# Windowed attention on one core: the softmax reciprocals go through GpSimd's DMA queue instead of SyncE's, the query loads move ahead of the key stores, and the block numbers are read one step earlier

## The reference, cut to what matters

```
logits = qd * SCALE @ jnp.swapaxes(kd, -1, -2)          # window means against window means
topk_logit, r_idx = jax.lax.top_k(logits, TOPK)         # TOPK = 4 block numbers for each window
kv_sel = kv_pix[jnp.arange(N)[:, None, None], r_idx]    # keys and values of those four windows
attn = jnp.einsum('npqhd,npkhd->nphqk', qh * SCALE, kh)
attn = jax.nn.softmax(attn, axis=-1)                    # over 4 * 64 keys
out = jnp.einsum('nphqk,npkhd->npqhd', attn, vh)
out = out + lepe                                        # a 3x3 depthwise convolution of v
out = out @ wo_w + wo_b
```

## Time and profile before

| | |
|---|---|
| median of three runs | 4997.75 us |
| the profiled execution | 4994.8 us, span 4993.0 us |
| attention with its loop | up to about 3640 us of the span |
| TensorE busy | 3844.4 us (77%), granted clock 0.86 on the mean |
| VectorE, ScalarE, GpSimd busy | 2436.6 (49%), 2310.0 (46%), 1249.2 us (25%) |
| DMA engines' mean busy share | between 0.2 and 0.5 in the attention |

### The profile page before, as it was taken

How to read it: one execution, slowest core, us unless ns; L and a number is a source line. 1 busy time by engine, 2 the same in 40 slices (tenths; PEclk the granted TensorE clock), 3 DMA queues, 4 the chain that set the end, 5 groups by cost and what they waited for, 6 DMA issues and landing times. The chain is left out here.

```text
span 4993.0 us, 164000 instructions
## 1 busy us (share of the span) xinstructions
PE 3844.4 (77%) x52926; PEld 2709.4 (54%) x52926; DVE 2436.6 (49%) x4011; ACT 2310.0 (46%) x5133; POOL 1249.2 (25%) x4158
## 2 busy tenths in 40 slices
PE   4246688678778777876877877788949799999889
PEld 1124455455445545544544554456612388888789
DVE  2254575475457447555745754576625233333311
ACT  1125565565556655555655555567713233333300
POOL 1012343243234324333432433344400000000000
PEclk9998898898888889888888888899955699999955
DMA  2323334333333333333333433343259543444486
GB/s 77 106 59 100 94 90 100 100 94 91 95 99 90 100 96 95 89 99 95 91 99 95 96 92 98 95 95 68 41 75 142 89 106 85 106 95 95 102 183 166
DMA packets 778337, 484.80 MB, mean 97 GB/s; under 512 B 483370, under 2 KB 752043, under 8 KB 773131
## 3 DMA queue, kind: packets, MB, share of 16 engines
q1 hardware_dynamic: 718210, 407.83, 36.5%
q10 hardware_dynamic: 59360, 67.44, 4.6%
HBM read 264.35 MB, written 209.19 MB: 95 GB/s over the span
## 5 line engine op out<-in xcount | busy, mean ns | idle before, releaser
L552 POOL COPY Ksel<-Kexp 96x128 int32 x3136 | 908.9, 332 | 1895.4 <-PE ps L1173 1406.8
L908 DVE TENSOR_REDUCE Mx<-ps 128x2 f32<-128x512 f32 x1568 | 1063.7, 688 | 526.7 <-PE ps L1151 520.3
L751 ACT ACTIVATE Pr<-ps 128x1024 f32<-128x1024 f32 x784 | 800.6, 1021 | 797.6 <-PE ps L1173 770.8
L681 ACT ACTIVATE Vsel<-Vpx 64x72 f32 x3136 | 818.3, 261 | 278.3 <-issue 144.1
L1171 PE MATMUL ps<-Qbd,Ksel 96*128 96x128 bf16 x6272 | 873.9, 229 | 21.2 <-issue 19.6
L1173 PE MATMUL ps<-MT,each 84*128 84x128 bf16 x6272 | 874.4, 229 | 0.0
L1151 PE MATMUL ps<-Ksel,Qbd 96*128 96x256 bf16 x3136 | 649.7, 291 | 170.3 <-POOL Ksel L552 125.5
L1171 PEld LDWEIGHTS ps<-Qbd,Ksel 96*128 96x128 bf16 x6272 | 646.2, 103 | 96.9 <-issue 87.6
L1173 PEld LDWEIGHTS ps<-MT,each 84*128 84x128 bf16 x6272 | 647.4, 103 | 90.4 <-issue 82.2
L1190 PE MATMUL ps<-Pr,Vsel 128*9 128x64 f32 x25088 | 538.2, 230 | 109.4 <-ACT O L689 99.6
L1190 PEld LDWEIGHTS ps<-Pr,Vsel 128*9 128x9 f32 x25088 | 392.2, 95 | 303.2 <-issue 302.1
(11 more groups left out here) (166 smaller groups left out, 3848.5 us busy)
## 6 DMA issues: line engine op xcount, KB each, us to landing
q_dram<-Pq SPq DMA_DIRECT2D x336, 112.0 KB
k_dram<-Pk SPq DMA_DIRECT2D x336, 112.0 KB
Kexp<-k_dram ACTq DMA_DIRECT2D x112, 336.0 KB, 5.2
Qbd<-q_dram SPq DMA_DIRECT2D x224, 168.0 KB, 4.8
Vpx<-v_dram ACTq DMA_DIRECT2D x112, 252.0 KB
s_dram<-S SPq DMA_DIRECT2D x8, 2048.0 KB, 12.7
Sin<-s_dram SPq DMA_DIRECT2D x32, 512.0 KB, 5.7
z_dram<-Zs SPq DMA_DIRECT2D x128, 128.0 KB, 4.1
```

Source lines behind the costliest of these rows:

```text
L552: nc.gpsimd.tensor_copy(dst[:, w, :, k, :], src[:, :, bass.ds(win[k] * (PX // 2), PX // 2)])\
L681: nc.scalar.activation(Vsel[par][half, w, k // 2], Vpx[b][half, bass.ds(win[k], 1)], ACT.Copy).then_inc(v_gathered, 1)
L751: nc.scalar.activation(Pr[k][:].rearrange("q c p h x -> q (c p h x)"), ps[:, ST0 + 2 * k:ST0 + 2 * k + 2, :].rearrange("q a b -> q (a b)") ...
L908: nc.vector.tensor_reduce(Mx[u % 2][:, 2 * half:2 * half + 2, w], ps[:, half, :].rearrange("q (p k) -> q p k", p=2), AX.X, ALU.max).then_i ...
```

## The change

Three edits, all in the attention:

* Steps 4 and 5 of the chain leave SyncE's program and stand in GpSimd's: the store after the gather of w = 2, the four loads ahead of the gather of w = 4 (behind `square`, ahead of `square2` and of the split of w = 5). SyncE's `sums_spread` now waits for the landing of the store of the unit before (`rsums_out`).
* In SyncE's slot `load_q` and `load_x` stand ahead of `store_k`.
* The register loads are functions of their own (`fetch_k`, `fetch_v`) and stand ahead of the wait for `st_ready`; on ScalarE that is also ahead of the exponential.

```
@@ sync engine @@
             def sums_spread(g, m):
                 hold(sp, "sp", o_copied, g * 2 + 2)
-                hold(sp, "sp", rsums_ready, g)
+                hold(sp, "sp", rsums_out, g * 16)
...
                 if behind:
                     store_q(e, u - 1)
-                if prev:
-                    rsums_to_dram(g - 1, (u - 1) % 2)
                 if behind:
                     store_vs(e, u - 1)
...
-                if behind:
-                    store_k(e, u - 1)
-                if prev:
-                    rsums_spread(g - 1, (u - 1) % 2)
                 if u < UNITS - 2:
                     hold(sp, "sp", st_ready, g * NWIN)
                     load_q(d, u + 2)
                 if not last and u < LAST:
                     load_x(e, u + 1)
+                if behind:
+                    store_k(e, u - 1)
@@ gpsimd @@
+            def fetch_k(u, w):
+                pool.load(regs, idxrow[0:1, u // NWIN, bass.ds((u % NWIN * NWIN + w) * TOPK, TOPK)])
+
+            def rsums_to_dram(g, m):
+                hold(pool, "pool", rsums_ready, g + 1)
+                pool.dma_start(rsums_dram[m].rearrange("j (p x) -> (j p) x", p=32), rsums[:, :]).then_inc(rsums_out, 16)
+
+            def rsums_spread(g, m):
+                hold(pool, "pool", rsums_out, g * 16 + 16)
+                hold(pool, "pool", on_ready, g)
+                for j in range(4):
+                    pool.dma_start(Rb[32 * j:32 * j + HD, :], rsums_dram[m, j].partition_broadcast(HD))\
+                        .then_inc(rb_loaded, 16)
...
+                    if w == 4 and prev:
+                        rsums_spread(g - 1, (u - 1) % 2)
...
+                        fetch_k((u + 2) % UNITS, w)
                         hold(pool, "pool", st_ready, g * NWIN + w + 1)
                         gather_k((u + 2) % UNITS, w)
+                    if w == 2 and prev:
+                        rsums_to_dram(g - 1, (u - 1) % 2)
                     if w == 3 and u <= LAST and not last:
                         square(e * NWIN + u, e * NWIN - 9 + min(u, 2))
                     if w == 4 and load is not None:
                         square2(load[0] * NWIN + load[1], e * NWIN + (0 if last else min(u, LAST) + 1))
@@ scalar engine @@
+                        fetch_v((u + 1) % UNITS, w)
                     hold(act, "act", st_ready, g * NWIN + w + 1)
                     hold(act, "act", pv_done, g * NWIN + w - 1)
...
```

More of the change, by code:

```diff
@@ L512, in _ @@
             sums_spread(duos * UNITS - 1, 1)
-            rsums_to_dram(duos * UNITS - 1, 1)
-            rsums_spread(duos * UNITS - 1, 1)
             store_u(d, NWIN - 2)
@@ L548, in gather_k @@
                 dst = Ksel[u % 2][:, :, :, :, :].bitcast(I32)
-                pool.load(regs, idxrow[0:1, b, bass.ds((u % NWIN * NWIN + w) * TOPK, TOPK)])
                 win = [pool.snap(r, min_val=0, max_val=WINDOWS - 1) for r in regs]
@@ L575, in _ @@
                 for w in range(NWIN):
+                    fetch_k(u, w)
                     gather_k(u, w)
@@ L583, in slot @@
                 load = late(d, u, first)
+                prev = not (first and u == 0)
                 for w in range(NWIN):
@@ L607, in _ @@
             bodies(pool, body)
+            rsums_to_dram(duos * UNITS - 1, 1)
             square2(tiles - 2, tiles)
+            rsums_spread(duos * UNITS - 1, 1)
             square2(tiles - 1, tiles)
@@ L671, in keep_v, with fetch_v @@
                                      ACT.Identity, bias=bv[:, 0:1]).then_inc(vs_ready, 1)
+            def fetch_v(u, w):
+                act.load(regs, idxrow[0:1, u // NWIN, bass.ds((u % NWIN * NWIN + w) * TOPK, TOPK)])
             def gather_v(g, u, w):
@@ L676, in gather_v @@
                 hold(act, "act", pv_done, (g - 2) * NWIN + w + 1)
-                act.load(regs, idxrow[0:1, b, bass.ds((u % NWIN * NWIN + w) * TOPK, TOPK)])
                 win = [act.snap(r, min_val=0, max_val=WINDOWS - 1) for r in regs]
@@ L725, in _ @@
             for w in range(NWIN):
+                fetch_v(0, w)
                 gather_v(0, 0, w)
@@ L747, in slot @@
                         inv_std2(load[0] * NWIN + load[1])
+                    if not (last and u == UNITS - 1):
+                        if w == 0 and u + 1 == NWIN:
+                            hold(act, "act", v_loaded[1], d * (16 * NWIN) + 16 * NWIN)
+                            hold(act, "act", idx_stored[1], d * 16 + 16)
+                        if w == 0 and u + 1 == UNITS:
+                            hold(act, "act", v_loaded[0], e * (16 * NWIN) + 16 * NWIN)
+                            hold(act, "act", idx_stored[0], e * 16 + 16)
+                        fetch_v((u + 1) % UNITS, w)
                     hold(act, "act", st_ready, g * NWIN + w + 1)
@@ L760, in slot @@
                     if not (last and u == UNITS - 1):
-                        if w == 0 and u + 1 == NWIN:
-                            hold(act, "act", v_loaded[1], d * (16 * NWIN) + 16 * NWIN)
-                            hold(act, "act", idx_stored[1], d * 16 + 16)
-                        if w == 0 and u + 1 == UNITS:
-                            hold(act, "act", v_loaded[0], e * (16 * NWIN) + 16 * NWIN)
-                            hold(act, "act", idx_stored[0], e * 16 + 16)
                         gather_v(g + 1, (u + 1) % UNITS, w)
```

## The result

The changed kernel takes 5225.31 us (median of four runs, 5217.19 to 5237.27) against 4998.07 for the kernel before: ratio 1.0449, 95% interval 1.0426 to 1.0472. It is 227 us slower where 138 faster was forecast, outside the range.

A forecast was written before the change was run, and what follows sets the result against it. TensorE was the engine to fill, with 49 storing units waiting for a late `Rb` behind key stores. 280 + 25 - 127 - 9 - 30 - 3 = 136 us gained, so 4860 us; 8 in 10 range 4680 to 5060.

The forecast's parts named there:

- The store has long landed (1771.1 + 1.35): Storing units: the reciprocals' store, issued by GpSimd until 1771.1, lands 1.35 us later, before the broadcast loads start at 1773.9.
- On a queue of their own they don't stand behind them, and I take 2.4: Storing units: broadcast loads, no longer behind the key stores, land 2.4 us after their last issue instead of 5.66.
- the rival of the DMA engines: Loads limited by the DMA engines, not their queue place: landing keeps 5.66 us, time about 5020; chance 0.12.
- c = 0.9: Price in us of one DMA issue on GpSimd; a tenth moves 50 us, and the sign turns at 1.17.
- rival of cheap issues: A DMA issue on GpSimd costs about 0.5 us, storing units hit their ceiling, time about 4705; chance 0.22.
- c would be near 0.7 and the sum some 70 us better: Price of a GpSimd issue if set only by the skill's first-byte times, about 1 us against 0.6.
- 3.1 us a unit: 41 late units with a second layer norm: GpSimd's store and loads delay `square2`, which TensorE's `variance2` awaits; 127 us lost.
- costed at nothing: Query and band loads ahead of the key stores, and register loads ahead of the waits, were given no cost.
- neither load is waited for now: SyncE's query and band loads: nothing waits for them in the kernel before, so moving them was given no cost.
- u = 8 and the last duo: Quiet u = 8 without a layer norm loses 1.3 us in 7 units, 9 us; the last duo loses 30 us.
- the stated alarm: The prediction is wrong outright if `Rb` still lands over 5 us after its last issue.
- interleaving is what puts four small transfers ahead of the rest of six large ones: Argument that on shared DMA engines the four broadcast loads pass the six key stores, against landing staying 5.66 us.

The follow-up runs named there:

- pool_bulk_behind: The changed kernel with SyncE's twelve query and key stores held back until that unit's reciprocals' store has landed, query loads in front; 5463.27 us.
- bulk_last: The kernel before, chain still on SyncE, with `store_q`, `store_vs` and `store_k` behind the chain, the query loads and the band load; 5199.13 us.
- spread_first: The kernel before with the four broadcast loads ahead of the six key stores in SyncE's queue; 4899.44 us.
- pool_only: The kernel before with only the reciprocals' store and broadcast loads moved to GpSimd's queue; query loads and register loads where they were; 5165.24 us.
- pool_and_loads: The kernel before with the chain moved to GpSimd and the query and band loads ahead of the key stores, without the register-load edit; 5154.71 us.
- after_band_later: The changed kernel with ScalarE issuing the load of a band of keys at w = 4 and not at w = 3; 5123.89 us.

## Why the prediction was wrong, point by point

- **"The store has long landed (1771.1 + 1.35)": failed, and it is the step that decided the sign together with the next.** 1.35 us was read in the quiet unit and carried into the storing ones. There the store starts 1.9 to 3.3 us after the last of the six query stores is issued, and it lands in 5.5 to 7.1 us (means of u = 1 to 7). With the stores held back it lands in 2.0 to 3.7 (pool_bulk_behind), issued by SyncE with the stores behind it in 1.3 to 2.1 (bulk_last, u = 1 to 6). The query stores ahead of it are not the whole of this: in spread_first they stand there too, and it is 2.4 to 4.5. Nor is it the query loads, since pool_only, where they come later, has 6.0 to 7.2. What the kernels on GpSimd add, the transfers that SyncE issues behind the store or GpSimd's own queue, was not separated. The trace of before already had the term: the store's own data packets end 2.9 to 4.4 us after its issue in storing units and 0.7 us after it in u = 10, and its list has SyncE waiting for this landing after 5 us of key stores.

```profile
SPq L285 <- DMA rsums_dram<-rsums: 76.5, 57, 3.0
```

- **"On a queue of their own they don't stand behind them, and I take 2.4": failed.** The landing after the last issue stayed at 5.2 to 5.4 us in five of the seven storing units, on their means (3.5 in u = 2, 4.6 in u = 7; before 5.4 to 5.8), which is the rival of the DMA engines. The working had the key stores start at about 1771 and the loads at 1773.9, so the key stores were first in it too; it counted only places in a queue. The 2.08 us of the earlier trace rows was right for quiet stretches: in the last duo of the changed kernel, where VectorE waits, it is 1.7 to 2.5. This rival's own sum, 5020, was still 205 us too low, since it left the store's landing at 1.35.
- The unit u = 4 closes with these terms. From the end of the store's issue to VectorE's start I had 8.8 us (1771.1 to 1779.9). The store landed 4.3 us later than GpSimd was ready for it by my working (7.1 against 2.8), the four issues took 2.0 instead of 3.6, and `Rb` landed in 5.8 instead of 2.4: 8.8 + 4.3 - 1.6 + 3.4 = 14.9, as measured.
- **c = 0.9: wrong in the good direction.** The row of the kernel after:

```profile
L548 POOL DMA_DIRECT2D Rb<-rsums_dram x448: 502/507/547, 374.0 to 3860.3; - x150
L542 POOL DMA_DIRECT2D rsums_dram<-rsums x112: 589/598/752, 366.9 to 3856.3; - x112
```

  An issue costs 0.51 us, near SyncE's 0.34 and not near a tensor operation. My rival of cheap issues had this right, and with it forecast 4705 (its own sum gives 4709): the cheapness was worth little, since in both units above the store's landing, and not the issues, decided when the loads could go. The text's "c would be near 0.7 and the sum some 70 us better" is mis-summed too: at its own 50 us a tenth that is about 100.
- **Late units, "3.1 us a unit": the mechanism held, the size did not.** TensorE waits for `square2` as said (4.30 us in u = 10, forecast about 3.5), and moving the loads behind it returns 117 us there. The price was 197 instead of 127 us: the store, "landed 1962.6" by the same 1.35 us, needs 3.0 to 3.6 us to land from GpSimd in u = 9 to 12 (1.9 to 2.0 with the band's load later, 1.3 to 1.6 from SyncE); and behind the gap TensorE runs on at half the clock.
- **What is late next, once one stall is gone:** I named no successor to the wait for `Rb` inside GpSimd. The split of the maxima follows the loads in its queue, and TensorE's transposition waits 173.2 us for it.
- **Register loads "costed at nothing": right alone, wrong together.** The text had them compete with the exponential; what they did was to let a 336 KB load past the store. Query loads at nothing: right (pool_only 5165, pool_and_loads 5155), though "neither load is waited for now" was not: the list of before has TensorE waiting for `Qbd` for 38.2 us in 8 cases (29.9 in the kernel after).
- u = 8 and the last duo: 23 and 44 us against 9 and 30. I put this down to the same two causes; no run was made for it.
- Of what would show it, the stated alarm came: `Rb` over 5 us after its last issue. The late units did lengthen (u = 10 to 29.8 us, about 27 forecast), and TensorE's wait for the product fell below 150 (131.7). Storing units at 28 us, and the wait for `Rb` under 250, did not come.

The Trainium skill (DMA: Bandwidth & Descriptors, Issuing engines are not separate DMA queues) says that DMAs of all engines run on the same 16 DMA engines and interleave. The landings agree: 5.2 to 5.4 us from GpSimd's queue, 5.4 to 5.8 from SyncE's behind six key stores. My argument against the rule, that "interleaving is what puts four small transfers ahead of the rest of six large ones", did not hold here: four small loads issued on another queue after the key stores landed hardly sooner than on the same queue, and much sooner only where the key stores were issued behind them (2.9 to 3.4 us in u = 2 of the change, 2.1 to 3.1 in spread_first).

Three things stay open. One is why the store lands later from GpSimd's queue than in spread_first, as said above. The second is the broadcast loads' landing of 5.2 us: that the key stores ahead of them make about 2 us of it is read from u = 2 and spread_first, but the rest was not split between the query stores, the band's load and others; in pool_bulk_behind, where the query stores start together with the loads, it is 3.1 to 4.2. And after_band_later is 41 us faster than edit 1 alone; part of that was the band in u = 9, where it left 0.72 us ahead of the store in five of seven duos in pool_only, but the rest was not taken apart.

## What to carry to other kernels

In this kernel a small transfer on a chain that is waited for was late mainly because of the large ones issued before it and around it, on whichever queue, and moving it to another engine's queue did not get it past them: first order the transfers by when they are needed (here loads whose inputs are ready at the head, the chain next, stores whose buffer is wanted soon, then the rest), and only then think of another queue. A landing time is to be read in the stretch where it will be used, and in a wait that is already in the list, not in the quiet unit next to it. A wait moved into the queue of an engine that computes holds up everything that engine has behind it, so its price is the landing together with the issue (here 256.7 us of waiting and 225.2 us of issuing loads); the prediction had reckoned with the issue alone.

## What the runs showed of the hardware that was not expected

- A DMA issue occupied GpSimd for 0.51 us (broadcast load, 28 KB) and 0.60 us (the reciprocals' store), SyncE for 0.34.
- From GpSimd the store needed at the least 1.8 us from the end of its issue to the first load that waits for it, where SyncE's took 1.3; the four loads landed 1.7 to 2.5 us after their last issue in the last duo, about as from SyncE (2.08 in the earlier trace rows).
- The order of two issues on two engines' queues, a few tenths of a microsecond apart, decides who waits: with the 336 KB load under 0.1 us ahead of the store or behind it the chain needs 2.5 to 2.9 us from the store's start to the first load (21 late units of pool_and_loads), with the load 0.3 us ahead 4.0 to 4.7 (u = 9 to 12 of the kernel after).
- After about 4 us without a matmul in a late unit the next pair of TensorE took 1.83 us instead of 0.99, and the granted clock was 0.70 on the mean of two microseconds in the gap, then 0.50, the lower of its two levels of 1.2 and 2.4 GHz, from 2054 to 2058.
